# One hybrid model on one core: which pair of heads the score matmuls of the first attention block take first

## The reference, cut to what matters

```
x = layernorm(x)
C_q  = x @ Wq_d + bq_d                    # 512 -> 12
C_kv = x @ Wkv_d + bkv_d                  # 512 -> 4
q = (C_q @ W_qk + b_qk).reshape(b, s, 32, 4)
scores = q . C_kv for each head           # 512 x 512 per head and sequence
attn   = softmax(scores)                  # not causal
v = C_kv @ Wv_u + bv_u                    # 32 heads of 16
out = (attn @ v) @ Wo + bo
```

## Time and profile before

| | |
|---|---|
| median of 3 runs | 2386.35 us (2382.11 to 2391.37) |
| the profiled execution's own time | 2382.11 us |
| its span, first to last instruction | 2380.4 us |
| PE matmul busy | 2160.6 us, 91% |
| DVE busy | 1409.8 us, 59% |
| ACT busy | 1112.9 us, 47% |
| mean granted TensorE clock | 0.96 |

### The profile page before, as it was taken

The page is one execution under the profiler, slowest core; times in us unless marked ns, Lnnn a source line. Parts: engine busy times, 40 slices in busy tenths (PEclk is TensorE's granted clock), DMA queues, the critical chain, the costliest instruction groups (busy, mean ns, idle before and its releaser), DMA issues. The chain is left out here.

```text
span 2380.4 us, 33455 instructions
## 1 busy us (share of the span) xinstructions
PE 2160.6 (91%) x11632; PEld 1489.4 (63%) x11632; DVE 1409.8 (59%) x2503; ACT 1112.9 (47%) x2671; POOL 722.2 (30%) x870
## 2 busy tenths in 40 slices
PE   6999898879999999999988689999999986899988
PEld 4333377656777777777765567666666664554457
DVE  5888574346656655666645455555555555657756
ACT  4677642224434444444434455554555533325553
POOL 2000002544444444444430222222222122346621
PEclk9899999989999999999999799999999987989999
DMA  2000023741111111111001343433432201453310
GB/s 88 1 1 1 22 89 100 163 98 54 32 40 54 32 40 54 31 39 34 19 36 47 104 103 87 107 85 93 107 83 67 60 23 53 156 92 72 67 36 36
DMA packets 112541, 149.18 MB, mean 63 GB/s; under 512 B 39588, under 2 KB 52516, under 8 KB 110200
## 3 DMA queue, kind: packets, MB, share of 16 engines
q1 hardware_dynamic: 64376, 108.77, 16.1%
q0 software_dynamic: 48000, 38.28, 7.0%
HBM read 86.07 MB, written 27.26 MB: 48 GB/s over the span
## 5 line engine op out<-in xcount | busy, mean ns | idle before, releaser
L1842 POOL TENSOR_TENSOR attn0b_probs<-attn0b_probs,attn0b_recip 128x128 f32<-128x128 f32 (+3 forms) x256 | 192.5, 772 | 223.4 <-DVE attn0b_recip L2081 223.3
L2540 ACT ACTIVATE attn1a_probs<-attn1a_scores,attn1a_negmax 128x128 f32<-128x128 f32 (+3 forms) x256 | 132.9, 524 | 180.6 <-DVE attn1a_negmax L2661 179.7
L1948 ACT ACTIVATE attn0b_probs<-attn0b_scores,attn0b_negmax 128x128 f32<-128x128 f32 (+3 forms) x256 | 132.8, 524 | 149.3 <-DVE attn0b_negmax L2074 148.0
L1956 ACT ACTIVATE attn0b_probsT<-attn0b_turned 128x128 f32<-128x128 f32 (+3 forms) x128 | 56.0, 438 | 243.5 <-PE attn0b_turned L2222 243.1
L2235 PE MATMUL attn0b_out<-attn0b_probsT,attn0b_v_now 128*128 128x512 f32 x320 | 153.9, 612 | 12.1 <-DVE attn0b_probsT L2088 12.1
L1468 DVE TENSOR_REDUCE attn0a_negmax<-attn0a_by_query 128x2 f32<-128x1024 f32 x128 | 152.1, 1219 | 11.7 <-PE attn0a_by_query L1555 11.6
L2661 DVE TENSOR_REDUCE attn1a_negmax<-attn1a_scores 128x2 f32<-128x256 f32 (+3 forms) x128 | 105.4, 824 | 77.9 <-PE attn1a_scores L2861 77.8
L2873 PE MATMUL attn1a_turned<-ident_f,attn1a_probs 128*128 128x128 f32 x640 | 115.4, 278 | 20.0 <-DVE attn1a_probsT L2669 18.0
L2074 DVE TENSOR_REDUCE attn0b_negmax<-attn0b_scores 128x2 f32<-128x256 f32 (+3 forms) x128 | 104.8, 819 | 46.4 <-PE attn0b_scores L2211 46.4
L37 PE MATMUL attn0b_aux<-attn0b_wo_hi,attn0b_oT_hi 128*128 128x512 f32 x256 | 125.7, 491 | 1.4 <-DVE attn0b_oT_lo L2092 1.4
L2222 PE MATMUL attn0b_turned<-ident_f,attn0b_probs 128*128 128x128 f32 x640 | 94.8, 275 | 23.1 <-POOL attn0b_probs L1842 21.7
(11 more groups left out here) (514 smaller groups left out, 6144.4 us busy)
## 6 DMA issues: line engine op xcount, KB each, us to landing
pre<-in_b_o SPq DMA_DIRECT2D x16, 1024.0 KB, 5.4
attn1a_qT<-attn1a_stage SPq DMA_DIRECT2D x128, 128.0 KB, 2.4
attn1a_qT<-attn1a_stage SPq DMA_DIRECT2D x64, 256.0 KB, 3.8
pre<-in_b_q SPq DMA_DIRECT2D x8, 1024.0 KB, 6.9
pre<-in_b_kv SPq DMA_DIRECT2D x5, 1024.0 KB, 6.1
attn0b_vals<-attn0b_v_out SPq DMA_DIRECT2D x16, 256.0 KB, 4.7
attn0b_keys_hi<-attn0b_part_hi POOLq DMA_DIRECT2D x32, 128.0 KB, 5.0
attn0b_keys_lo<-attn0b_part_lo POOLq DMA_DIRECT2D x32, 128.0 KB, 7.7
```

What stands on the lines that cost most here:

```text
L1842: pool.tensor_tensor(x, x, recip[:, r % 2, e:e + 1].broadcast_to([P, (qt + 1) * P]), ALU.mult).then_inc(s_scaled, 1)
L1948: act.activation(probs[:, r % 2, e, 0:width], scores[r % 2][:, e, 0:width], ACT.Exp, bias=negmax[:, r % 2, e:e + 1], accum_out=sums[:, r % ...
L2540: act.activation(probs[:, r % 2, e, 0:width], scores[r % 2][:, e, 0:width], ACT.Exp, bias=negmax[:, r % 2, e:e + 1], accum_out=sums[:, h % ...
```

## The change

Both functions that turn a unit's number g into a query tile and a pair of heads take the pairs in the other order. Before, unit 0 of a query tile is heads 2 and 3 (a = 1) and unit 1 is heads 0 and 1. After it, unit 0 is heads 0 and 1, and unit 1 is heads 2 and 3. Nothing else differs.

```diff
@@ in the vector engine's program
             def maximum(step, g):
-                qt, a = g // 2, 1 - g % 2
+                qt, a = divmod(g, 2)
                 dve.wait_ge(s_by_query, NG * step + g + 1)
```

## The result

The changed kernel takes 2404.74 us in the median of 8 runs (2396.54 to 2418.18), against 2386.57 (2382.11 to 2391.37, 8 runs): a ratio of 1.0078 with a 95% interval of 1.0059 to 1.0096, or +14 to +23 us. The forecast was 2400.5, slower, in a range of 2392 to 2411.

The account below looks back on a forecast made before the run. TensorE, 91% busy, was taken to set the pace together with waits on ScalarE and VectorE. Exposed conflicts, 12.0 + 0.9 + 1.4 = 14.3 us on the median 2386.35, gave 2400.7; predicted 2400.5, range 2392 to 2411.

Parts of the forecast that it names:

- One conflict, 0.23 us: On TensorE, each four queues two deep on its row groups, adding 0.23 us at full clock, weight load hidden.
- Rival 3: The load of a busy row group is not hidden: 0.33 us per conflict, about +22 us, 2408; chance 0.10.
- Four of eight come through, 0.92 us per step: Conflicts in g = 7, 0, 1, 4 are exposed at 0.23 us each; those in g = 5, 6, 2, 3 otherwise absorbed or shared.
- VectorE's path through the reciprocal: The maximum that g = 7's scores await also comes 0.23 us late, so g = 5 to 7 cost +0.23, not +0.46.
- Rivals 1 and 2: First: more absorbed or cheaper conflicts, +5 to +11 us, chance 0.15. Second: row group does not matter, +0, chance 0.06.
- Only the order of row groups matters: Banks, semaphores, waits, shapes and counts stay; only row groups move; VectorE's and ScalarE's instructions cost the same, +0.
- The idle time before the zeros of g = 3: TensorE's wait for ScalarE's o_sb absorbs two conflicts, 0.46 us, and shrinks from 0.56 to about 0.1 us.
- 12.0 + 0.9: Exposed conflicts in us: 13 periods from step 2's g = 0 to step 15's, then four more in step 15.
- The clock, costed at nothing: The granted clock stays at 1.00 after 76 us in the steady steps, so no cost was added for it.
- estimate for step 1: At half clock four exposed conflicts cost 1.7 us, about 0.3 comes back as the clock rises: 1.4 us.
- Rival 4: The clock falls for a stretch of some 20 us, costing about 9 us on top, 2410; chance 0.04.

Follow-up runs that it names:

- x12: On top of the change, both score matmuls of a unit read the first head's row group, so one group gets three matmuls: 2456.52 us, ratio 1.0293.
- x8: Kernel before with the units reordered so that same-group pairs fall only in g = 2 and 5: 2388.15 us, ratio 1.0004.
- x10: Kernel before with the units reordered so that same-group pairs fall only in g = 2 and 7: 2388.76 us, ratio 1.0007.
- x9: Kernel before with the units reordered so that same-group pairs fall only in g = 1 and 4: 2398.85 us, ratio 1.0040.
- x11: Kernel before with the units reordered so that same-group pairs fall in g = 2, 5, 6 and 7: 2395.87 us, ratio 1.0035.
- x2: On top of the change, scores_by_key and exponential flipped too, so each four again uses four row groups: 2387.28 us, ratio 0.9998.
- x3: On top of the change, scores take heads 0,2 then 1,3, so each four shares one row group instead of two: 2404.50 us, ratio 1.0076.
- x1: The changed kernel again with no edit, run beside the kernel before: 2410.86 us, ratio 1.0094.
- x5: Kernel before with the changed order in steps 3 to 15 alone: 2399.42 us, ratio 1.0042.
- x6: Kernel before with the changed order in steps 0 to 2 alone: 2392.52 us, ratio 1.0022.
- x4: Kernel before plus 8 more zero matmuls in g = 1 from step 2 on, 0.88 us: 2398.29 us, ratio 1.0046.
- x7: Kernel before plus three zero matmuls in every iteration of step 0 and in g = 0 to 2 of step 1: 2395.03 us, ratio 1.0034.

## Why the prediction was right, and by how much it was short

**One conflict, 0.23 us: right.** 0.67 against 0.44 in g = 5, and again 0.23 for the third place in x12. The Trainium skill, "TensorE: Matmul & The Clock Gate", Part 3, The mechanism, says in one sentence that a weight load overlaps with running matmuls only when the row group differs (another sentence of the section also allows it into a background weight buffer). The loads of the changed kernel overlap on the same row groups (154.63 to 154.82, under the by_key matmuls that started at 154.52), so here the measurement decides against the first sentence. Rival 3, the load that is not hidden, falls by the same rows.

**Four of eight come through, 0.92 us per step: right.** 14.39 - 13.48 = 0.91. The places were tested in small sets: g = 2 and 5 (x8), g = 2 and 7 (x10) cost nothing, g = 1 and 4 cost 0.46 (x9), and g = 5, 6, 7 (with the absorbed g = 2) together cost 0.23 (x11). That g = 0 costs its 0.23 and g = 3 nothing is read from the changed kernel's timeline alone: from g = 0 to g = 1 the pairs are 2.73 us apart (159.03 to 161.76) where they were 2.50, and 0.34 of the pause is left. VectorE's path through the reciprocal is read there too (1.64 against 1.41); x11 does not test it, since by the same rows TensorE's own queue in g = 6 and 7 would give about the same 0.23. Rivals 1 and 2 fell here.

**Only the order of row groups matters: right** (x2), and it is the fullest group that counts (x3), a point that the prediction had not made.

**The idle time before the zeros of g = 3: short.** I expected about 0.1 and found 0.34. In g = 2 and in g = 3 the two by_key matmuls had been 0.10 to 0.12 us apart before (158.61 with 0.60 in the earlier trace rows, and the row of g = 3 below), and they start together now (0.50 at 163.54). So the two conflicts took 0.22 from the pause, not 0.46. It costs nothing either way. Before:

```profile
160.15 0.62 PE L1569 MATMUL attn0a_by_key<-attn0a_shifted,attn0a_keys 32*128 32x512 f32 x2
```

**The sum, term by term.** L1540 turns the maxima in g = 0 of a step, so its rows mark the steps. These are the ones of steps 1, 2 and 16, first of the kernel before, then of the changed one:

```profile
58.11 1.11 PE L1540 MATMUL attn0a_aux<-ident_f,attn0a_negmax 128*128 128x128 f32 x4
74.55 0.66 PE L1540 MATMUL attn0a_aux<-ident_f,attn0a_negmax 128*128 128x128 f32 x4
...
262.94 0.66 PE L1540 MATMUL attn0a_aux<-ident_f,attn0a_negmax 128*128 128x128 f32 x4
```

```profile
57.41 1.11 PE L1540 MATMUL attn0a_aux<-ident_f,attn0a_negmax 128*128 128x128 f32 x4
73.88 0.66 PE L1540 MATMUL attn0a_aux<-ident_f,attn0a_negmax 128*128 128x128 f32 x4
...
274.65 0.66 PE L1540 MATMUL attn0a_aux<-ident_f,attn0a_negmax 128*128 128x128 f32 x4
```

From step 2 to step 16 the change costs 200.77 - 188.39 = 12.4 us, where 12.0 + 0.9 were counted (the 13 periods give 11.7, step 15 gives 0.7). Step 1 costs 0.03 us (16.47 against 16.44), where 1.4 were counted, and the block's first L1540 comes 0.7 earlier, which together makes the 11.7 us by which the next block starts later. In x1 step 1 costs 2.2 us and step 2 costs 6.9.

**The clock, costed at nothing: the term that was mis-sized.** The sum was 14.3, the median difference 18.2 (14 to 23 by the interval), and 24 on x1's chip. The steady steps are indeed at 1.00 in both profiles of the changed kernel. What failed is the estimate for step 1, 1.4 us with the clock rising no later than before. It rises at 70 us in one execution of the changed kernel and at 92 in another, against 74 in the profile of before. Split by steps, 13 of the 15 cost 11.7 us (x5) and the early ones 4.8 (x6), where 1.4 and one step's 0.9 had been counted. A delay of equal size without shared groups costs 11.5 in all (x4). In the profiles the low stretch that begins at 47 to 50 us ended by 74 us in all six kernels without shared groups in steps 1 and 2, or with them in two absorbed places only (before, x2, x4, x5, x8, x10). Of the seven others with them (changed, x1, x3, x6, x9, x11, x12), four went on to between 79 and 92. (x7, whose zeros are another thing, ended at 76.)

Fourteen profiles are few, but the record has the mean granted clock of every execution. With 0.50 and 1.00 as the levels that the windows show, a mean c over a span s stands for 2 x (1 - c) x s us at 0.50. Averaged over the executions of each kernel (standard errors 1 to 4 us):

| kernel | executions | us at 0.50 in the whole span |
|---|---|---|
| before | 71 | 198 |
| x2, x4, x8, x10 | 12, 6, 10, 10 | 197, 198, 198, 198 |
| x5 (changed order from step 3 on) | 6 | 193 |
| changed (all its executions on record), x1 | 25, 4 | 205, 219 |
| x6 (changed order in steps 0 to 2) | 12 | 210 |
| x3, x9, x11 | 6, 10, 10 | 211, 207, 210 |
| x7 (zeros, no shared groups) | 12 | 208 |
| x12 | 4 | 312 |

Over the 71 executions of before, a microsecond more at 0.50 goes with 0.37 us more time. By that estimate the changed kernel's 7 us more are worth 2.5, which with the 14.3 makes 16.8 of the 18.2, and x6's 12 us more are worth 4.4. So the longer time at the low clock is real. It comes with the kernels that lose time in steps 1 and 2, and x5 lacks it. Rival 4 had such a stretch on top of the queueing, at 9 us; it came with a few us in the median. Two things are not shown. x7 has no shared groups in these steps and stays low 10 us longer too, so it may be any delay or added work of TensorE there, and not the sharing of row groups; no run has an equal delay without zeros or shared groups in steps 1 and 2. And why the stretch is longer in one execution and not in another is open.

No version came out faster than the kernel before.

## What to carry to other kernels

When small matmuls run side by side on different row groups, look at which instruction stands next to which across functions: an innocent renumbering of heads in one of them can put two on the same rows, and each place in the queue costs one stream. To price it, follow one period and ask at each place what ends the next wait; half of these conflicts cost nothing, because something else was being waited for there. Give the clock a price of its own where the block starts at the low level: here the kernels that lost time in steps 1 and 2 stood 7 to 22 us longer at that level (x12 far longer).

## What the runs showed of the hardware

- Four matmuls of 32 rows and 512 columns on four row groups start within 0.01 us, and the next operation follows 0.43 to 0.44 us behind them; on two groups, two deep, 0.66 to 0.67 (changed kernel, x3, x10); with one group three deep, 0.89 (x12). At the low clock matmuls on one row group come 0.43 us apart.
- The weight load of a row group whose matmul is still running was hidden (changed kernel: 0.19 us, from 0.11 us behind that matmul's start).
- I had not expected queueing on row groups to go along with a lower granted clock. With three deep (x12), TensorE's rows are busy for all of the time shown (4.00 of 4 us) and the clock still falls to 0.50 in steady steps; in x9 it fell once, to 0.57 over 4 us, also at 4.00 busy. The busy time of these rows does not tell the two levels apart.
